# DLRM tower on one core: both factors of the pair products read from SBUF, with new first steps, folds and output layout

## The reference, cut to what matters

```python
e = jnp.stack([tbl_0[ids[:, 0]], ..., tbl_15[ids[:, 15]]], axis=1)   # 2048 samples, 16 fields, 256 numbers each
# three layers; x = e, and xk = x in the first:
for i in range(3):
    z = jnp.einsum('bfe,bge->bfge', x, xk).reshape(B_, F_ * F_, E_)
    z = jnp.swapaxes(z, 1, 2)
    z = jnp.einsum('bcl,oc->bol', z, Ws[i]) + bs[i][None, :, None]
    z = jax.nn.relu(z)
    z = jnp.sum(z, axis=-1)
    outs.append(z)
    xk = jnp.broadcast_to(z[:, :, None], (B_, F_, E_))
h = concatenate([outs..., dense_ctx])           # 48 + 16 columns
h = relu(h @ W_top1 + b_top1)                   # 512
h = relu(h @ W_top2 + b_top2)                   # 256
y = h @ W_top3                                  # 1
```

## Time and profile before

| What | Value |
|---|---|
| Three runs | 577.11, 577.75 and 579.12 us, median 577.75 |
| Profiled execution | 575.6 us |
| Its span | 573.8 us |
| Granted PE clock | 1.00 |
| PE busy | 538.3 us (94%) |
| DVE busy | 536.5 us (94%) |
| POOL busy | 460.0 us (80%) |
| ACT busy | 403.5 us (70%) |
| DMA engines | 20.4% of 16 engines' span on the gathers, 63 GB/s on average |

### The profile page before, as it was taken

One profiled execution on the slowest core, in us unless ns is written; L12 is line 12 of the kernel. 1 busy time (PEld: TensorE's weight loads), 2 busy tenths in 40 slices (PEclk: granted clock), 3 DMA queues, 4 the chain that ended last, 5 costly groups with the idle time before them and its releaser, 6 DMA issues.

```text
span 573.8 us, 17766 instructions
## 1 busy us (share of the span) xinstructions
PE 538.3 (94%) x7488; PEld 323.8 (56%) x7488; DVE 536.5 (94%) x248; ACT 403.5 (70%) x1214; POOL 460.0 (80%) x562
## 2 busy tenths in 40 slices
PE   1877989999999999999999999999999999999997
PEld 0333445565656656565665666656566656656565
DVE  4799899999999999999999999999999999999852
ACT  3465766877768587776858777685877768687743
POOL 5899999897988989798898979889897988977100
PEclk9999999999999999999999999999999999999999
DMA  3522222222222222222222122222222222221000
GB/s 89 139 75 71 69 66 66 71 61 67 65 66 65 67 65 58 67 65 67 66 66 67 57 66 66 66 65 67 66 59 65 67 65 67 65 67 38 2 1 2
DMA packets 16881, 35.98 MB, mean 63 GB/s; under 512 B 7969, under 2 KB 8353, under 8 KB 16801
## 3 DMA queue, kind: packets, MB, share of 16 engines
q0 software_dynamic: 12288, 33.57, 20.4%
q1 hardware_dynamic: 4514, 1.29, 1.0%
HBM read 34.84 MB, written 0.01 MB: 61 GB/s over the span
## 4 chain that ended last, share of the span: by engine, by line
DVE 34%; issue 24%; ACT 17%; PE 16%; POOL 9%; DMA 0%; ACTq 0%; DVEq 0%; SPq 0%; POOLq 0%
DVE prods L212 25%; ACT relu_k L496 8%; PE sum_ps L629 7%; DVE relu_k L371 6%; POOL emb L252 5%; ACT relu L486 3%; PE sum_ps L644 2%; POOL prods L262 2%; PE turn_ps L609 2%; ACT emb_t L468 2%; POOL prods L212 2%; ACT emb_t L469 1%; DVE z_cat L377 1%; PE outer_ps L732 1%; DVE own_sum L350 1%
## 5 line engine op out<-in xcount | busy, mean ns | idle before, releaser
L212 DVE TENSOR_TENSOR prods<-turn_ps,emb_t 128x3360 f32<-128x3360 f32 x128 | 462.2, 3642 | 11.2 <-ACT emb_t L469 11.2
L252 POOL DMA_INDIRECT emb<-tables,rows_sb x256 | 251.6, 983 | 44.8 <-issue 37.9
L629 PE MATMUL sum_ps<-prods,w_sb 128*32 128x272 f32 x4096 | 266.8, 398 | 8.7 <-POOL prods L212 8.7
L629 PEld LDWEIGHTS sum_ps<-prods,w_sb 128*32 128x32 f32 x4096 | 126.3, 110 | 101.5 <-issue 13.8
L486 ACT ACTIVATE relu<-sum_ps,bias_sb 128x120 f32<-128x120 f32 x256 | 92.0, 373 | 104.0 <-PE sum_ps L629 104.0
L262 POOL TENSOR_TENSOR prods<-emb_t 128x256 f32<-128x256 f32 x128 | 95.0, 742 | 32.2 <-ACT emb_t L469 30.4
L468 ACT COPY emb_t<-turn_ps 128x512 f32<-128x512 f32 x128 | 75.9, 593 | 44.5 <-PE turn_ps L609 44.5
L609 PE MATMUL turn_ps<-ident_sb,emb 128*128 128x128 f32 x512 | 85.7, 291 | 19.8 <-DMA emb<-tables,rows_sb 10.0
L609 PEld LDWEIGHTS turn_ps<-ident_sb,emb 128*128 128x128 f32 x512 | 54.8, 143 | 66.9 <-issue 31.1
L496 ACT ACTIVATE relu_k<-outer_ps 128x2048 f32<-128x2048 f32 x44 | 83.4, 1896 | 2.3 <-PE outer_ps L702 2.3
L476 ACT ACTIVATE prods<-emb_t 128x512 f32<-128x512 f32 x128 | 83.8, 655 | 0.1
(11 more groups left out here) (90 smaller groups left out, 296.4 us busy)
## 6 DMA issues: line engine op xcount, KB each, us to landing
emb<-tables,rows_sb POOLq DMA_INDIRECT x256, 2.8
w_sb<-w_top SPq DMA_DIRECT2D x1, 512.0 KB, 4.3
w_sb<-w_top SPq DMA_DIRECT2D x1, 256.0 KB, 5.4
ids_sb<-ids_t SPq DMA_DIRECT2D x1, 128.0 KB, 2.1
z_cat<-dense_b SPq DMA_DIRECT2D x1, 128.0 KB, 3.9
ident_sb<-ident SPq DMA_DIRECT2D x1, 64.0 KB, 2.1
w_sb<-w_cols SPq DMA_DIRECT2D x1, 64.0 KB, 2.1
wp_sb<-w_proj SPq DMA_DIRECT2D x1, 32.0 KB, 1.7
```

What stands on the lines that cost most here:

```text
L212: eng.tensor_tensor(out, every, shifted, ALU.mult).then_inc(done, 1)
L252: nc.gpsimd.indirect_dma_start(out=emb[:, k % EMB_RING, t * E:(t + 1) * E], out_offset=None, in_=tables, in_offset=bass.IndirectOffsetOnAx ...
L629: last = nc.tensor.matmul(sum_ps[s * 2 * F:(s + 1) * 2 * F, k % 2, 0:SUM_COLS], w_sb[:, c, odd, :], x[:, c, 2 * s + odd, :, :], start=c == ...
```

## The change

1. DVE's products (`products`) read the block's own fields from `emb_t`, as POOL's do. Both inputs of that instruction are in SBUF then.
2. The first steps: SP loads ids and limits in one, and the bias rows before the identity; DVE makes the row numbers of the first 8 tiles ahead of the others; the first tile of step 0 is turned into a PSUM bank of its own and multiplied on its own (`first_tile`, `take_first_tile`), steps 2 and 3 are turned into banks of `outer_ps`, three steps are turned ahead at the start in place of two; LEAD is 3 in place of 4.
3. `relu_pairs` computes relu(2x + 2b) for the pairs and puts the sum as a 17th column into `own0`, so that `finish0` is one reduction over 17 columns.
4. The folds add two halves of 128 columns into one another, so that `reduce_fields` reads 128 elements in place of 256. The folds at the very end (`end_fold`) stay.
5. The last layer has samples on the partitions: `h2` is the weight operand and `w3_sb` the moving one, one column; `y` leaves as 128 x 16 and is turned on the host.

```diff
-LEAD = 4
+LEAD = 3
+FIRST_ROWS = 4 * PAIR
...
+        def turned_rows(k):
+
+            if k in (2, 3):
+                return outer_ps[:, k - 2, :]
+            return turn_ps[:, k % 2, :]
+
+        def first_tile():
+
+            return outer_ps[:, 2, 0:E]
...
             sp.dma_start(ids_sb[:], ids_t).then_inc(ids_in, 16)
-            sp.dma_start(id_lim[:], id_limits).then_inc(ids_in, 16)
-            sp.dma_start(ident_sb[:], ident).then_inc(consts_in, 16)
+            sp.dma_start(bias_in[:], bias_rows).then_inc(bias_in_done, 16)
+            sp.dma_start(parts_sb[:], bias_parts).then_inc(bias_in_done, 16)
+            sp.dma_start(ident_sb[:], ident).then_inc(ident_in, 16)
...
             def half_shift(k):
 
                 if k < STEPS:
+                    if k == 0:
+                        pool.wait_ge(emb_t_first, 2)
...
-            dve.wait_ge(ids_in, 2 * 16)
-            nc.vector.tensor_copy(id_lim_f[:], id_lim[:]).then_inc(setup, 1)
+            dve.wait_ge(ids_in, 16)
+            most, offset = (ids_sb[:, TILES + n:TILES + n + 1].bitcast(FP32) for n in range(2))
+            nc.vector.tensor_scalar(rows_sb[:, 0:FIRST_ROWS], ids_sb[:, 0:FIRST_ROWS], 0.0, most, ALU.max, ALU.min).then_inc(setup, 1)
...
             def products(k):
 
                 if k < STEPS:
+                    own = emb_blocks(k)[:, :, 0:F]
+                    first = 0
+                    if k == 0:
+                        first = BLOCKS // PAIR
+                        dve.wait_ge(emb_t_first, 2)
+                        multiply(nc.vector, k, 0, first, own[:, 0:first, :], prods_first)
                     dve.wait_ge(emb_t_ready, 2 * (k + 1))
                     at_least(dve, sums_done, k - PRODS_RING + 1)
-                    own = turn_ps[:, k % 2, :].rearrange("p (n f) -> p n f", f=F)[:, 0:VECTOR_BLOCKS, :]
-                    multiply(nc.vector, k, 0, VECTOR_BLOCKS, own, prods_dve)
+                    multiply(nc.vector, k, first, VECTOR_BLOCKS, own[:, first:VECTOR_BLOCKS, :], prods_dve)
 
             def finish0(g):
 
                 dve.wait_ge(relu0_ready, 3 * PER * (g + 1))
-                nc.vector.tensor_reduce(own_sum[:], own0[:, g % 2, :, :], AX.X, ALU.add).then_inc(own_sum_ready, 1)
-                dve.wait_ge(own_sum_ready, g + 1)
                 at_least(dve, diag_ready, g - 1)
-                nc.vector.scalar_tensor_tensor(out=z0_rows[:, g % 2, :], in0=pair_sum[:, g % 2, :], scalar=2.0,
-                                               in1=own_sum[:], op0=ALU.mult, op1=ALU.add).then_inc(z0_ready, 1)
+                nc.vector.tensor_reduce(z0_rows[:, g % 2, :], own0[:, g % 2, :, :], AX.X, ALU.add).then_inc(z0_ready, 1)
...
-                                        outer_ps[:, FOLD_BANK[k], 0:F * F].rearrange("p (f o) -> p o f", o=F),
+                                        outer_ps[:, FOLD_BANK[k], 0:P].rearrange("p (f o) -> p o f", o=F),
...
+                                             bias=bias_twice[:, 0:1], scale=2.0,
+                                             accum_out=own0[:, g % 2, PAIR * i + t, F:F + 1]).then_inc(relu0_ready, 1)
...
-                    if k < 2:
-                        wait_gathered(k)
-                    at_least(pe, prods_dve, k - 1)
+                    if k < 4:
+                        if k == 0:
+                            pe.wait_ge(gathered_first, 16)
+                        else:
+                            wait_gathered(k)
+                    else:
+                        pe.wait_ge(prods_dve, k - 1)
...
-                    last = nc.tensor.matmul(out, w3_sb[:, i:i + 1], h2[:, g % 2, i * P:(i + 1) * P], start=i == 0, stop=i == H2 - 1)
+                    last = nc.tensor.matmul(out, h2[:, g % 2, i * P:(i + 1) * P], w3_sb[:, i:i + 1], start=i == 0, stop=i == H2 - 1)
...
-                    for j in range(J):
-                        last = nc.tensor.matmul(outer_ps[j * R:(j + 1) * R, FOLD_BANK[k], 0:F * F], fold_sb[:],
-                                                relu_k[:, k, q // HALF_G, j, q % HALF_G, :], start=q == first, stop=q == G4 - 1)
+                    for half in range(2):
+                        for j in range(J):
+                            last = nc.tensor.matmul(outer_ps[j * R:(j + 1) * R, FOLD_BANK[k], 0:P], fold_sb[:],
+                                                    relu_k[:, k, q // HALF_G, j, q % HALF_G, half * P:(half + 1) * P],
+                                                    start=(q, half) == (first, 0), stop=(q, half) == (G4 - 1, 1))
```

More of the change, by code:

```diff
@@ L146, in build @@
         ids_in = sem("ids_in")
+        ident_in = sem("ident_in")
         consts_in = sem("consts_in")
@@ L465, in take_turned, with take_first_tile @@
                     at_least(act, proj_done, old // PER + 1)
-                    src = turn_ps[:, k % 2, :].rearrange("p (n f) -> p n f", f=F)
+                    src = turned_rows(k).rearrange("p (n f) -> p n f", f=F)
                     out = emb_blocks(k)
-                    nc.scalar.copy(out[:, :, 0:F], src).then_inc(emb_t_ready, 1)
-                    nc.scalar.copy(out[:, :, F:WRAP], src[:, :, 0:F // 2]).then_inc(emb_t_ready, 1)
+                    half = BLOCKS // PAIR if k == 0 else 0
+                    nc.scalar.copy(out[:, half:, 0:F], src[:, half:, :]).then_inc(emb_t_ready, 1)
+                    nc.scalar.copy(out[:, half:, F:WRAP], src[:, half:, 0:F // 2]).then_inc(emb_t_ready, 1)
+            def take_first_tile():
+                act.wait_ge(turned_first, 1)
+                src = first_tile().rearrange("p (n f) -> p n f", f=F)
+                out = emb_blocks(0)[:, 0:BLOCKS // PAIR, :]
+                nc.scalar.copy(out[:, :, 0:F], src).then_inc(emb_t_first, 1)
+                nc.scalar.copy(out[:, :, F:WRAP], src[:, :, 0:F // 2]).then_inc(emb_t_first, 1)
             def squares(k):
                 if k < STEPS:
+                    if k == 0:
+                        act.wait_ge(emb_t_first, 2)
                     act.wait_ge(emb_t_ready, 2 * (k + 1))
@@ L542, in relu_half @@
                 nc.scalar.activation(relu_k[:, k, q, 0:2, :, :].rearrange("p j h n -> p j (h n)"), src, ACT.Relu).then_inc(end_relu_act, 1)
-            for k in range(2):
+            take_first_tile()
+            for k in range(3):
                 take_turned(k)
@@ L553, in _ @@
                     relu_hidden1(g)
-                take_turned(slot + 2)
+                ahead = 3 if slot == 0 else slot + 2
+                if slot != 1:
+                    take_turned(ahead)
                 if slot == STEPS - 1:
@@ L559, in _ @@
                     take_side(slot, *SIDE_AT[slot])
-                squares(slot + 2)
+                if slot != 1:
+                    squares(ahead)
             relu_hidden2(LAST - 2, 0, sum_ps[:, 0, SIDE])
@@ L608, in turn @@
                             wait_sums_read(k - 2)
-                        last = nc.tensor.transpose(turn_ps[:, k % 2, i * P:(i + 1) * P], emb[:, k % EMB_RING, i * P:(i + 1) * P],
+                        out = first_tile() if k == 0 and i < EC else turned_rows(k)
+                        last = nc.tensor.transpose(out[:, i * P:(i + 1) * P], emb[:, k % EMB_RING, i * P:(i + 1) * P],
                                                    ident_sb[:])
@@ L669, in side @@
                 else:
-                    output(g, sum_ps[0:1, slot % 2, SIDE])
+                    output(g, sum_ps[:, slot % 2, SUM_COLS + F:SUM_COLS + F + 1])
             def outer_round(k, g, q):
@@ L753, in _ @@
             turn(1)
-            wait_gathered(2)
+            turn(2)
+            pe.wait_ge(consts_in, N_CONSTS * 16)
             h1_banks = (outer_ps[:, H1_BANK, :], outer_ps[:, H1_BANK + 1, :])
@@ L762, in _ @@
                     pe.wait_ge(top_in, N_TOP * 16)
-                turn(slot + 2)
+                if slot == 0:
+                    turn(3)
+                    pe.wait_ge(prods_first, 1)
+                if slot < 2:
+                    pe.wait_ge(prods_dve, slot + 1)
+                else:
+                    turn(slot + 2)
                 if slot in SIDE_AT:
@@ L815, in _ @@
             wait_end_relus(1, LAST, 0)
-            output(LAST - 2, outer_ps[0:1, 2, 0:P])
+            output(LAST - 2, outer_ps[:, 2, 0:1])
             turn_features(PREV, outer_ps[:, 1, 0:P])
@@ L832, in _ @@
             hidden2(LAST, 1, outer_ps[:, 2, 0:P])
-            output(PREV, sum_ps[0:1, 0, 0:P])
-            output(LAST, sum_ps[0:1, 0, P:2 * P])
+            output(PREV, sum_ps[:, 0, 0:1])
+            output(LAST, sum_ps[:, 0, 1:2])
 def shape_constants():
```

66 lines of the change are left out of this document (37 added, 29 removed).

## The result

The changed kernel takes 952.9 us (median of four runs, 950.9 to 953.2) against 577.4 before. The ratio is 1.649, with a 95% interval of 1.645 to 1.653: 65% slower. The forecast was slower, 858 us, with a range of 600 to 1040; the sign and the mechanism came out, and its size was 95 us short.

What follows compares the result with a forecast made beforehand. DVE and PE were taken as full, POOL near it, DVE leading PE by 1.6 us. Profiled 575.6 + 285 for the held beat - 5 at the start = 856, 858 on the median; range 600 to 1040, its own 800 to 960.

Steps and rivals of the forecast that it cites:

- Operand, exclusion: DVE's two-SBUF product and POOL's two reading products exclude each other, for the full 3.64 us of a product.
- The step I called weakest: The symmetry: POOL waits behind a whole DVE product, though the trace showed only DVE waiting for POOL.
- 0 for the product itself: DVE's product costs the same with both inputs in SBUF: 0, bounds 2 us either way for 128.
- The beat by hand: DVE, POOL and PE steps worked through: 6.40 us a step against 4.18, +285 us over 128.
- if gathers are held as well: Upper bound: POOL asks four times a step, 7.1 us a step, with PE's part 8, or +490 us.
- rival (c): Worse: gathers held too, or PE's clock falling back to its lower level; 1065 us; chance 0.09.
- rival (a): POOL's half shift and last blocks fit DVE's gaps: 5.3 us a step, 716 us against the median; chance 0.13.
- PE's clock: PE's new waits might bring back its lower clock, as in the first sums, 3.86 us against 2.04 later.
- The signs: DVE's product mean above 3.7 us or idle before it; POOL's products starting at product ends; PE near 65% busy.
- Folds: PE's 96 narrow matmuls replacing 48 wide ones cost +1.4 us a group, bounds 0 and 2.9.
- Start: Earlier gathers and first turn, LEAD 3: 5 us saved, bounds 2 and 7; first sums near 15 us.
- Rival (d): No exclusion for this product, PE binds: 570 us on the median, 561 with DVE binding; chance 0.17.

Runs made afterwards that it cites:

- the control: Kernel before with DVE's products reading both inputs from SBUF, rows loaded by SP's plain DMAs, POOL's two products replaced by fills: 583.0 us.
- the one-line kernel: Kernel before with one line changed, DVE's products reading the block's own fields from the SBUF copy: 952.4 us, one of four runs at 913.9.
- half products: Kernel before with the SBUF operand, and DVE's product split into two instructions of 15 blocks: 880.1 us.
- the run with fills: Kernel before with the SBUF operand, and both of POOL's products replaced by fills that read nothing, gathers kept on POOL: 794.3 us.
- the run with SP's loads: Kernel before with the SBUF operand, and SP loading consecutive table rows by plain DMAs in place of POOL's gathers, POOL's products kept: 719.5 us.
- the version with the PSUM operand: Changed kernel with only the operand undone, DVE's products reading own fields from PSUM again: 566.9 us, 0.984 of the kernel before.

## Why the prediction was right, and where its size was off

**Operand, exclusion.** Right, in both directions. The step I called weakest, that POOL stands still behind a whole product, by symmetry, holds: 405.58 above for a reading product, 397.68 for a gather. 0 for the product itself holds as well: 3657 ns in the control against 3642, 15 ns each, 1.9 us for 128, at the edge of my 2. The 8 us that the Trainium skill's fixed parts (VectorE: DVE Perf Modes, the section on the TRN2 errata) would save did not come; the sign was the other.

**The beat by hand.** This is the mis-sized term: +285 us, measured +376 (the one-line kernel). I let the gathers run free under the product, and the free gathers let the beat recover between holds. The upper bound of the same paragraph, "if gathers are held as well", gave 7.1 a step before PE's part. The z0 reductions of the changed kernel start from 73.6 to 924.9 us:

```profile
L375 DVE TENSOR_REDUCE z_rows<-own x16: 428/436/437, 73.6 to 924.9; 128x16 f32<-128x272 f32 x16
```

15 groups of 8 steps in 851.3 us are 7.09 a step (the last of them, in which the gathers run out, took 44.2 us, the others 56.5 to 57.9). Times 128 and against 4.18 that is +373. So the case to forecast was a part of rival (c), with the row for it in hand: L353 at 116.08 stood still until the gather ended. I wrote that it allowed held gathers and put 0.09 on it. The other part of (c), that PE's work adds to 8 a step, did not come: the chain has POOL at 70% and PE at 7%. That the time fell within my forecast's own 800 to 960 is partly luck: the beat that I summed gives 858, and with 7.1 in its place the same sum gives 946.

A simpler sum than the beat is POOL's own time plus one hold for each product, as long as POOL has work waiting. 3.63 for a step's list, 0.3 for the z products and 3.2 make 7.1. With half products the holds are 2.6 and the sum 6.5, as measured (781.7 us for 120 steps). The 3.2 is no constant: in the run with fills, which pass under a product, the holds are 2.6 us a product, and 2.9 of list, 0.3 and 2.6 make 5.8, where 5.9 was measured and a hold of 3.2 would ask for 6.4. With 1.35 us of list, 4.9 is less than the 5.3 of taking turns, and the run with SP's loads came at 719 us where rival (a)'s 5.3 gave 716.

**PE's clock.** The half of rival (c) that concerned it came true, though it decided little. In the middle of the changed kernel PE's granted clock averages 0.81, and sums differ by what PE did before (window, then two rows of PE's timeline):

```profile
400.00:450.00 50.00, 34.15 (x450) 19.99 (x446) 26.92 (x12) 21.28 (x66) 47.37 (x34) 0.81 0.14 41
```

```profile
404.47 2.04 PE L676 MATMUL sum_ps<-prods,w_sb 128*32 128x272 f32 x32 [1.44 <-POOL prods L226]
406.33 1.93 PE L772 MATMUL outer_ps<-relu_k,fold_sb 128*32 128x128 f32 x64
...
414.97 3.86 PE L676 MATMUL sum_ps<-prods,w_sb 128*32 128x272 f32 x32 [5.78 <-POOL prods L226]
```

After 5.78 us of waiting the same 32 matmuls take 3.86 us at the lower level, 1.2 GHz (granted clock 0.50 from 414.90 to 418.80); after 1.44 us they take 2.04 at 2.4 (1.00 from 404.00 to 406.50). That is 1.8 us, mostly in places where POOL sets the pace: PE has 7% of the chain, 67 us, and the low clock can account for a part of them. No experiment took it apart.

**The signs.** I had named 65% of PE busy in the middle as a sign: 34.15 of 50 is 68%. The mean of DVE's product above 3.7 us came too, 3.85. One sign looked otherwise than I had written: a held instruction of POOL shows as a long record (4.22 us), not as idle time before it, which is 4.2 and 2.2 us in all for the half shifts and the last blocks.

**Folds.** Wrong in sign: +1.4 us a group forecast, measured a gain of 2.3 us over the kernel. 64 narrow matmuls take 1.93 us above, as 32 wide ones did. The lower bound, 0, was the right value for PE, and DVE's shorter reductions (266 in place of 396 ns, 28 times, 3.6 us) would be enough for the gain; nothing separated the two.

**Start.** 5 us forecast. In the version with the PSUM operand the first sums came at 18.20, as late as before, not near 15. The first gather (3.87) and the first turn (7.44) came 0.5 and 1.2 us sooner, nearly as I had it, and LEAD 3 alone brings the first sums of the kernel before to 15.64, by just the 2.5 us that I gave it. What failed is their sum: with three steps turned ahead, turn 3 stands ahead of the first sums in PE's list and waited 2.98 us for the gathers of step 3. By the first z0 reduction the start had brought 2.1 us (47.2 against 49.3); the larger part of the 9.1 came from the groups, 32.9 us in place of 33.4, where I had priced 0.2. LEAD 3 has a share in that, 0.3 a group, which I had not priced. Rival (d)'s 570 for the whole change without exclusion, against 566.9 measured, was near for partly wrong reasons.

## What to carry to other kernels

Before an operand of a DVE instruction is moved from PSUM to SBUF, count its SBUF inputs and look at what POOL does meanwhile: with two, DVE and POOL's reads and gathers take turns, instruction by instruction, and a kernel in which both are nearly full loses on POOL, for each such DVE instruction, 3.2 us of 3.66 here and 1.3 of 1.9 with half products. A tiny instruction with a scatter in its durations (16 elements, 0.17 to 0.97 us) is a cheap witness of such an exclusion, and each of its delayed instances should be matched with what POOL ran and ended, gathers too. A pipeline in which POOL has about 0.5 us of room a step (44.09 of 50 us busy) also pays for work put ahead of it at the start: two gathers fewer were 3 to 5 us, of which 2.5 can be followed in the traces as POOL's earlier start.

## What the runs showed of the hardware

- A gather issued by POOL, 0.98 us alone, is held by a DVE product with two SBUF inputs and ends 0.86 us behind it; with nothing else on POOL that reads in a step, gathers averaged 2.26 us. The Trainium skill (SBUF — State Buffer, Who interferes with whom) infers that descriptor generation needs the write interface of the shared pair, so that a DVE tensor_tensor, which takes only the read interface, would leave it alone. These runs show otherwise for indirect DMAs. Such a gather also reads its row numbers from SBUF (`rows_sb`), and no run separates that from the making of the descriptors; plain DMAs from POOL were not tried.
- Fills on POOL were not held: 326 and 301 ns on average, 337 at most, with 105 of them begun inside two-input products of 3.66 us. There the same section of the Trainium skill, which has GpSimd instructions that only write go free, agrees.
- Neither side goes first for long: with work waiting on both, DVE and POOL alternated, three and three in 12.27 us. One exception is in the changed kernel: a product whose record starts at 190.72 waited for POOL's last blocks and for the z_wide that followed them at once, and took 5.04 us.
- A hold ends with the DVE instruction that is running: with products of 3.66 us POOL's longest half shift took 4.22 us, with halves of 1.9 us 2.46.
